# A graph network's attention hops: the first tile of every group gathered by TensorE from the table in SBUF instead of by an indirect DMA

## The reference, cut to what matters

```
h = concat(emb[head], emb[tail]) @ fc_w.T + fc_b
e = leaky_relu(sum(h * relation_emb[type]), slope 0.2)
w = softmax of e over the edges of each head
emb = sum over the edges of a head of w * emb[tail]  + emb
emb = emb / norm(emb)
```

## Time and profile before

| | us |
|---|---|
| time, median of 3 runs | 8048.83 (8046.11 to 8049.55) |
| the profiled execution: time | 8066.15 |
| the profiled execution: span | 8064.3 |
| TensorE busy (matmul) | 5613.4 (70%) |
| VectorE busy | 5187.3 (64%) |
| ACT busy | 1729.5 (21%) |
| GpSimd busy | 5810.4 (72%) |

### The profile page before, as it was taken

One profiled execution on the slowest core, in us unless ns is written; L12 is line 12 of the kernel. 1 busy time (PEld: TensorE's weight loads), 2 busy tenths in 40 slices (PEclk: granted clock), 3 DMA queues, 4 the chain that ended last, 5 costly groups with the idle time before them and its releaser, 6 DMA issues. The chain is left out here.

```text
span 8064.3 us, 179296 instructions
## 1 busy us (share of the span) xinstructions
PE 5613.4 (70%) x42094; PEld 3878.4 (48%) x42095; DVE 5187.3 (64%) x25581; ACT 1729.5 (21%) x3898; POOL 5810.4 (72%) x5647
## 2 busy tenths in 40 slices
PE   0991699999001477777777767777777777488885
PEld 0110111111000377766777656777777676366664
DVE  6888655555001577777777767777777777555555
ACT  2000000000000233333333323333333333122221
POOL 0888877777777577777777747777777777277775
PEclk9995899999555555555555555555555555588997
DMA  2992577776001333333323333323333333233332
GB/s 68 305 309 62 152 245 244 243 244 206 4 4 21 84 79 79 79 79 78 78 79 79 78 62 80 79 78 79 79 79 78 79 79 79 36 68 68 69 69 53
DMA packets 494534, 828.90 MB, mean 103 GB/s; under 512 B 225634, under 2 KB 379257, under 8 KB 445197
## 3 DMA queue, kind: packets, MB, share of 16 engines
q10 hardware_dynamic: 76307, 411.51, 15.4%
q0 software_dynamic: 180560, 257.90, 15.0%
q1 hardware_dynamic: 237610, 158.84, 7.9%
HBM read 800.05 MB, written 19.90 MB: 102 GB/s over the span
## 5 line engine op out<-in xcount | busy, mean ns | idle before, releaser
L1133 POOL DMA_INDIRECT rows<-tab_d,stage_idx x3264 | 3105.5, 951 | 1102.6 <-issue 992.0
L218 POOL DMA_INDIRECT rec_d<-stage_rec,stage_row x1600 | 1957.3, 1223 | 673.3 <-issue 662.3
L1183 PE MATMUL ps_g<-rows,prob 128*128 128x65 f32 x6528 | 1571.7, 419 | 8.9 <-issue 3.8
L427 PE MATMUL ps_gate<-ring,h_sb 128*1 128x512 f32 x3072 | 1488.4, 593 | 0.2 <-issue 0.2
L1183 PEld LDWEIGHTS ps_g<-rows,prob 128*128 128x128 f32 x6528 | 1440.8, 325 | 70.9 <-issue 40.2
L1467 POOL DMA_INDIRECT y_rows<-y_d,stage_src x768 | 736.6, 959 | 372.6 <-issue 217.7
L1149 PE MATMUL ps_turn<-ident_b,s_parts 128*128 128x128 bf16 x816 | 233.3, 286 | 972.8 <-DVE s_parts L1276 972.3
L1164 PE MATMUL ps_p<-ident_f,prob_t 128*128 128x128 f32 x3264 | 876.5, 423 | 0.0
L628 DVE TENSOR_SCALAR lo_hot<-iota_b,lo_t 128x128 bf16<-128x128 bf16 x1568 | 484.7, 324 | 461.1 <-PE ps_deg L438 439.5
L1264 DVE SCALAR_TENSOR_TENSOR picked<-iota_f,typ_e,x_sum 128x50 f32<-128x50 f32 x3264 | 698.5, 270 | 123.6 <-DVE x_sum L1261 107.5
L1241 DVE CUSTOM_DVE_ANT_0 masked<-lower,ps_s,m_old 128x512 f32<-128x512 bf16 x816 | 610.3, 748 | 162.5 <-DVE m_old L1239 155.0
(11 more groups left out here) (290 smaller groups left out, 6874.1 us busy)
## 6 DMA issues: line engine op xcount, KB each, us to landing
ring<-w_ih ACTq DMA_DIRECT2D x192, 1024.0 KB
ring<-w_hh ACTq DMA_DIRECT2D x192, 1024.0 KB
lo_wide<-lo_d SPq DMA_DIRECT2D x816, 128.0 KB
rows<-tab_d,stage_idx POOLq DMA_INDIRECT x3264
rec_e<-list_lo_d SPq DMA_DIRECT2D x216, 128.0 KB
rec_d<-stage_rec,stage_row POOLq DMA_INDIRECT x1600
y_rows<-y_d,stage_src POOLq DMA_INDIRECT x768
rec_d<-blank ACTq DMA_DIRECT2D x1, 3584.0 KB, 32.6
```

Of the source, the lines that this page charges most:

```text
L218: pool.indirect_dma_start(out=rec_d, out_offset=bass.IndirectOffsetOnAxis(ap=stage_row[:, h, j:j + 1], axis=0), in_=stage_rec[:, h, j, :], ...
L427: mm = pe.matmul(ps_gate[:, s, :], lhsT=h_sb[:, kc:kc + 1], rhs=ring[:, pc % RING, q, :], start=(kc == 0), stop=(kc == KC - 1))
L1133: pool.indirect_dma_start(out=rows[:, h * 4 + g, k, :], out_offset=None, in_=tab_d[hop], in_offset=bass.IndirectOffsetOnAxis(ap=stage_idx[ ...
L1183: mm = pe.matmul(ps_g[:, p, 0:C + 1], lhsT=prob[:, p, k * P:(k + 1) * P], rhs=rows[:, u, k, 0:C + 1], start=(k == 0), stop=(k == KT - 1))
```

## The change

In both hops the first tile of each group is no more fetched by an indirect DMA. The table's 115 used columns are kept in SBUF as three bf16 parts too (`t_parts`, built in `Tables`). In the stage before the hops VectorE finds, for each group, the first block of tails that its first tile reaches (`group_first`), and codes each tail relative to it: the place in the block plus 128, times a power of two for the block, in four scaled copies, stored beside the index rows in `lo_d` (so `lo_wide` has two rows, 256 KB). It also finds how many sweeps of four blocks (`GW`) the widest group takes (`n_near`).

In a hop VectorE compares the four code rows with the code of each partition, which gives the one-hots of four blocks at once (`hot_near`), in an inner loop over the sweeps. TensorE zeroes the accumulator `ps_t` and adds 4 blocks x 3 parts of the table in the same inner loop (`gather`), and ACT copies the result into the first tile of `rows`. The zeroing matmul and the gather are first in TensorE's order.

Further: scores stay float32, one operation instead of five, and are spread by four float32 turns of a broadcast column. ACT makes the mask, by Abs with a scale and a bias. All scores are negated, so that the running maximum is a minimum and the exponential takes it as its bias. There is one more lag, the index rows are asked for four groups ahead over two semaphores, and several buffers are laid over memory that is free by then.

```diff
-LAGS = (0, 1, 2, 3, 4)
+LAGS = (0, 1, 2, 3, 4, 5)
-LO_AHEAD = 3
+LO_AHEAD = 4
-PER_GROUP = 12
+PER_GROUP = 8
...
+    GW = 4
+    TW = C + 1 + R
+    MAX_NEAR = -(-NB // GW)
+    NBW = MAX_NEAR * GW
...
@@ Tables.vector @@
+    for lo, hi in ((0, half_cut), (half_cut, NB)):
+        t = tab[:, lo:hi, 0:TW]
+        rest = ...
+        link(dve.tensor_copy(t_parts[:, lo:hi, 0, :], t))
+        link(dve.tensor_tensor(rest, t, t_parts[:, lo:hi, 0, :], ALU.subtract))
+        link(dve.tensor_copy(t_parts[:, lo:hi, 1, :], rest))
+        link(dve.tensor_tensor(t_parts[:, lo:hi, 2, :], rest, t_parts[:, lo:hi, 1, :], ALU.subtract))
...
@@ the stage before the hops @@
+    for w in range(MAX_NEAR):
+        link.mark(dve.tensor_scalar(node_code[:, w:w + 1], part_f[:], float(P), 2.0 ** (GW * w), ALU.add, ALU.mult))
...
+    link(dve.scalar_tensor_tensor(out=near_rows[:, :, 0, :], in0=near_lo, scalar=float(P), in1=near_i.bitcast(F32),
+                                  op0=ALU.add, op1=ALU.mult))
+    for w in range(1, GW):
+        link.mark(dve.tensor_scalar(near_rows[:, :, w, :], near_rows[:, :, 0, :], 2.0 ** -w, None, ALU.mult))
...
@@ SP in a hop @@
-    wait_tick(sp, tick, lo_in, g * 16)
-    wait(sp, lower_rdy, g - 7)
-    sp.dma_start(lo_wide[:, u % 8, :], lo_d[ds(g, 1), :].broadcast_to([P, GE])).then_inc(lo_in, 16)
+    wait_tick(sp, tick, lo_in[u % 2], rows_in(g, u) - 16)
+    wait_tick(sp, tick, lower_rdy, g - 7)
+    wait(sp, hot_t_rdy, g - 7)
+    sp.dma_start(lo_wide[:, u % 8], lo_d[:, ds(g, 1), :].rearrange("v g e -> g v e")
+                 .broadcast_to([P, 2, GE])).then_inc(lo_in[u % 2], 16)
...
@@ GpSimd in a hop @@
-    for k in range(KT):
+    for k in range(1, KT):
...
@@ TensorE in a hop @@
+    def gather(g, first):
+        wait(pe, kept, g)
+        pe.matmul(ps_t[:, 0:TW], lhsT=zero_t[:], rhs=zero_t[:, 0:TW], start=True, stop=True,
+                  skip_group_check=True)
+        with pe.bass.Fori(0, sweeps, 1, engines=(pe.engine,)) as w:
+            at = pe.snap(pe.bass.s_assert_within(first + w * GW, 0, NBW - GW, ...))
+            pe.wait_ge(near_rdy, sweeps * g + (w + 1))
+            for b in range(GW):
+                for j in range(3):
+                    mm = pe.matmul(ps_t[:, 0:TW], lhsT=hot_near[:, b, :],
+                                   rhs=t_parts[:, ds(at + b, 1), j, :].rearrange("p a c -> p (a c)"),
+                                   start=False, stop=(j == 2), skip_group_check=True)
+            mm.then_inc(gathered, 1)
     def spread(g, p):
-            mm = pe.matmul(ps_s[:, p, k * P:(k + 1) * P], lhsT=pick_k[:, k, :], rhs=s_rows[:, p, :], ...)
+            mm = pe.transpose(ps_s[:, p, k * P:(k + 1) * P],
+                              score[:, p, k:k + 1].broadcast_to([P, P]), ident_f[:])
...
+    def body(i, u, stages, block_of, first_of):
+        _, z, a, s, _, c = stages
+        if z: gather(i - 1, first_of(1))
+        if s: spread(i - 3, (u - 3) % 2)
+        if c: turn_prob(i - 5, (u - 5) % 2)
+        if a: scores(i - 2, u % 2, (u - 2) % 8, block_of(2))
+        if c: sums(i - 5, (u - 5) % 2, (u - 5) % 8)
...
@@ ACT in a hop: the order is copy of the gathered tile, copy of the probabilities, exponential, mask @@
+        if z:
+            act.wait_ge(gathered, act_sweeps * g + (act_sweeps + 1))
+            act.activation(rows[:, v, 0, 0:TW], ps_t[:, 0:TW], ACT.Copy).then_inc(kept, 1)
...
+            act.activation(lower[:, (u - 1) % 4, :], lo_wide[:, (u - 1) % 8, 0, :], ACT.Abs,
+                           bias=far_bias[:], scale=BIG).then_inc(lower_rdy, 1)
...
@@ VectorE in a hop: masked minimum, m_diff, m_run, hot_t, x_sum, picked, score, hot_near, acc @@
+            link(dve.tensor_tensor_reduce(masked[:, p, :], lower[:, (u - 4) % 4, :], ps_s[:, p, :], 1.0,
+                                          m_old[:, p:p + 1], ALU.add, ALU.min, m_new[:, p:p + 1]))
+            dve.tensor_tensor(m_diff[:, p:p + 1], m_new[:, p:p + 1], m_old[:, p:p + 1], ALU.subtract
...
+            g, q = i - 2, u % 2
+            wait(dve, kept, g + 1)
+            wait(dve, landed[(u - 2) % 8], (g - (u - 2) % 8) * (PER_LAND // 8) + PER_LAND)
             wait(dve, x_rdy, g + 1)
...
+            dve.scalar_tensor_tensor(out=score[:, q, :], in0=s_raw[:, q, :], scalar=0.2,
+                                     in1=s_raw[:, q, :], op0=ALU.mult, op1=ALU.min).then_inc(score_rdy, 1)
+        if w:
+            wait(dve, lo_in[u % 2], rows_in(i, u))
+            dve.sem_inc(dtick, 1)
+            with dve.bass.Fori(0, sweeps, 1, engines=(dve.engine,)) as t:
+                dve.wait_ge(gathered, sweeps * i + (t + 1))
+                dve.tensor_scalar(hot_near[:].rearrange("p b e -> p (b e)"), lo_wide[:, u % 8, 1, :],
+                                  node_code[:, ds(t, 1)], None, ALU.is_equal).then_inc(near_rdy, 1)
```

More of the change, by code:

```diff
@@ L88, with pipelined @@
 BLOCK_LEAD = 8
-LAGS = (0, 1, 2, 3, 4)
+LAGS = (0, 1, 2, 3, 4, 5)
 LAG = LAGS[-1]
 UNROLL = 8
-LO_AHEAD = 3
-def pipelined(eng, n, body, table=None, top=0, link=None):
+LO_AHEAD = 4
+def pipelined(eng, n, body, tables=(), link=None):
     def steps(i0, count, flags):
-        v = blocks_from(eng, table, i0, UNROLL if count == UNROLL else 0, top) if table is not None else None
+        found = [(blocks_from(eng, table, i0, UNROLL if count == UNROLL else 0, top, back), back)
+                 for table, top, back in tables]
         for u in range(count):
-            body(i0 + u, u, flags(u), (lambda d, u=u: v[BLOCK_BACK + u - d]))
+            body(i0 + u, u, flags(u), *((lambda d, u=u, v=v, back=back: v[back + u - d]) for v, back in found))
     steps(0, UNROLL, lambda u: tuple(u >= lag for lag in LAGS))
@@ L202, in gnn_kernel @@
         tick = sem("tick")
-        staged = [sem(f"staged{h}") for h in range(2)]
+        staged = sort_staged = [sem(f"staged{h}") for h in range(2)]
+        idx_ld = sem("idx_ld")
+        piece_ld = [sem(f"piece_ld{i}") for i in range(RING)]
+        STAGED_BEFORE, PIECES_BEFORE, IDX_BEFORE = ES // 32 * 32, 2 * RC * (PC // RING) * 16, 3 * 16
         scattered = [sem(f"scattered{h}") for h in range(2)]
@@ L917, in _ @@
                     mm.then_inc(turned_rdy, 1)
+                    if r == 1:
+                        pe.wait_ge(near_in, 1)
+                        for c in range(4):
+                            mm = pe.transpose(ps_near[0:GN, c, :], dst0[:, c * GN:(c + 1) * GN], ident_f[:])
+                        mm.then_inc(near_out, 1)
+                pe.wait_ge(near_in, 2)
+                for j, v in enumerate((first4, last4)):
+                    for c in range(4):
+                        mm = pe.transpose(ps_first[:, j, c * GN:(c + 1) * GN], v[:, c:c + 1].broadcast_to([GN, P]),
+                                          ident_f[0:GN, 0:GN])
+                mm.then_inc(near_out, 1)
                 pe.wait_ge(to_turn, 3)
@@ new lines, in gather @@
+                        def gather(g, first):
[3 more added lines that the diff above has]
+                            with pe.bass.Fori(0, sweeps, 1, engines=(pe.engine,)) as w:
+                                at = pe.snap(pe.bass.s_assert_within(
+                                    first + w * GW, 0, NBW - GW, skip_runtime_bounds_check_because=
+                                    "the first block is held so low that the last sweep ends in the table"))
+                                pe.wait_ge(near_rdy, sweeps * g + (w + 1))
+                                for b in range(GW):
+                                    for j in range(3):
+                                        mm = pe.matmul(ps_t[:, 0:TW], lhsT=hot_near[:, b, :],
+                                                       rhs=t_parts[:, ds(at + b, 1), j, :]
+                                                       .rearrange("p a c -> p (a c)"),
+                                                       start=False, stop=(j == 2), skip_group_check=True)
+                                mm.then_inc(gathered, 1)
@@ L1178, in sums @@
                         def sums(g, p, u):
-                            wait(pe, landed[u], (g - u) * 8 + 64)
+                            wait(pe, landed[u], (g - u) * (PER_LAND // 8) + PER_LAND)
                             wait(pe, prob_rdy, g + 1)
@@ L1418, in gnn_kernel @@
                                    "gathered", "got_rdy", "win_rdy", "spread_out", "tab_new"))
-            staged = [seml(f"staged_y{h}") for h in range(2)]
+            staged = sort_staged
             landed = landed_y
-            lo_in = [seml(f"list_lo_in{i}") for i in range(3)]
+            lo_in = piece_ld[0:3]
             AHEAD = 5
```

273 lines of the change are left out of this document (158 added, 115 removed).

## The result

| | before | after |
|---|---|---|
| time, median of 4 runs each, us | 8048.64 (8046.11 to 8049.55) | 9985.21 (9984.70 to 9986.38) |
| ratio, 95% interval | | 1.2407 (1.2385 to 1.2428) |
| span of the profiled execution | 8064.3 | 9984.6 |
| TensorE, VectorE, GpSimd busy, us | 5613, 5187, 5810 | 7265, 4951, 5030 |
| x_sum, first to last start, us | 2712.9 to 6901.2 | 2735.6 to 8833.3 |

The change makes the kernel 24% slower; 7600 us was predicted, with a range that ended at 8120. All of it but 11 us lies in the stretch from the first to the last x_sum (6097.7 us instead of 4188.3).

What follows compares the result with a forecast made beforehand. GpSimd's gathers were taken to bound the hops at 5.03 us a group; the new cycle gives 4.46. 8066 - 460 + 11 = 7617, less 17 for the median, so 7600 us; eight-in-ten range 7330 to 8120.

Steps and rivals of the forecast that it cites:

- one sweep: Inner loop in the hops: one sweep of four blocks holds the first 128 edges of every group.
- no table loads on ACT in a hop: ACT's mask by Abs needs no table of its own; the rival of table switches, 8100 to 8450 us, had 0.03.
- the cycle named: In a hop: hot_near waits for the previous group's scores, TensorE's gather follows, and the next x_sum waits for its scores.
- x_sum to score: VectorE's stretch from x_sum to score in each group, a term of the cycle: 1.41 us.
- the sum of the cycle: Per group in the hops, VectorE and TensorE terms at the high clock: 4.21 us, 4.46 with loop edge and clock dips.
- TensorE's gather at 12 x 0.05 = 0.60 us: Cycle term at the high clock: 12 of 13 matmuls, the zeroing being ahead of the wait.
- 2.4 GHz nearly throughout: TensorE's clock in the hops: high with dips at loop edges, granted clock above 0.85; dips cost 0.05 us a group.
- slow rival: TensorE's clock stays low in the hops: 6.07 us a group with the edge, about 8900 us; chance 0.10.
- o: Inner loop setup on VectorE between score and the comparison hot_near: 0.30 us a group.
- the handover to TensorE: Cycle term from VectorE's comparison to TensorE's gather: 0.05 us a group.
- The loop edge: Edge of the unrolled loop in the hops: 1.6 us once in eight groups, 0.20 us a group.
- Outside the hops: Table parts before hop 2 cost 3 us, one more pipeline step per hop 8 us, preparation of codes 0: 11 us.

Runs made afterwards that it cites:

- The filler: Changed kernel with the gather's zeroing matmul issued 13 times instead of once, in TensorE's gap before the gather: 9229 us, 1.146 of the kernel before.
- the repaired kernel: Changed kernel with hot_near ahead of x_sum in VectorE's order and register table loads in fours, everything computed: 7826 us, 0.972 of the kernel before.

## Why the prediction was wrong, point by point

**Right.** GpSimd was the bound before; one sweep; no table loads on ACT in a hop; the other parts of the change free; the cycle named, its members and what each waits for. x_sum to score took 1.42 us (1.41 forecast), and the index rows land 3.4 us after their issue (median), asked for four groups ahead (`LO_AHEAD`; the prediction has seven), and hold up nothing.

**The step that failed first: the sum of the cycle, TensorE's gather at 12 x 0.05 = 0.60 us.** It takes 1.83 in the changed kernel and 1.81 with the clock high. With a fixed address it takes 0.65. I took the price of a matmul from the four of the spread (ps_s), whose addresses are fixed, halved it for the high clock, and gave it to each of the 12 gather matmuls, which has a run-time address of its own. They start 0.13 us apart at either clock, and the spread follows 0.35 us behind the last one (0.13 with the inner loop written out, so 0.22 of the 1.83 is the loop's). The price also hangs on the place. In the kernel with hot_near first, in the 200 of 284 groups (3000 to 4500 us) where the sums are still running ahead of the gather and the clock is high, the first five or six gather matmuls start 0.05 us apart and the rest 0.12 to 0.14, with single steps up to 0.20. The filler's run has both prices in one kernel, 1.81 us behind a wait and 1.25 without one. That the address work is done ahead of time where the queue is full, and not where it stands at a wait, is my reading; it fits all of these numbers.

**The clock.** "2.4 GHz nearly throughout" followed from 5.57 us of TensorE work in a 4.46 us group. But the cycle leaves a gap whenever VectorE's score stretch is longer than the sums, and TensorE's work has to fit between. In 120 of 201 groups the clock stayed low; in the rest the high level stood at the sums and the gap, and the part that the cycle waits for was low but for short stretches. The filler prices this: spread, turn, scores and their handover 2.58 us low, 1.50 high, 1.08 us a group. My slow rival had the sign and this part of the mechanism, with a chance of 0.10, and was still 1070 us short, as it had the gather at 1.24, the inner loops at 0.30 and the edge at 0.20 a group. The Trainium skill (TensorE: Matmul & The Clock Gate, Part 1, "HAM oscillation") tells of a kernel whose batches of matmuls, with a DMA wait between them, each start at the low clock. The trace has the same outcome behind shorter waits as well (0.2 to 1.2 us inside a pass): spread and turn stood at 0.50 in all 201 groups. The rule that I did weigh, that turns keep the full clock from engaging (the Trainium skill, the same page, Part 4), is not what happened: with eight turns a group the repaired kernel has 0.94.

**The inner loops.** o was 0.30 us from score to hot_near; it is 0.48 to 0.59, and the handover to TensorE 0.23 instead of 0.05. Both include what I left out: o also holds score's own 0.16, and TensorE's loop has a setup of its own (with it written out the handover is 0.14). Together they are 0.47 us above the forecast in the group shown.

**The loop edge.** Forecast 1.6 us a pass, as the earlier trace rows; it is 3.75 (10.7 less 6.9), 0.47 a group instead of 0.20. I took for granted that a load of 9 to 13 entries costs what one of 12 does; the start of the load decides. The Trainium skill (Runtime: NRT & Kernel Launch, Instruction fetch mechanics) gives about 200 ns a register for a TENSOR_LOAD, even in bulk; it speaks of loads from HBM, and these tables lie in SBUF. The loads of the changed kernel are near that (2.40 us for 10, 0.24 each), those of the kernel before are not (0.85 for 12, 0.07 each).

The terms add up: gather +1.23, clock +1.08, loops +0.47 and x_sum to score +0.01 make the 7.00 us of the group shown out of 4.21; the mean inside a pass is 6.9, and with the edge's 0.47 it is the 7.4 measured.

**Outside the hops.** Forecast +11 us. Hop 1's first gather starts 14.5 us later (2721.1; the earlier trace rows), so the preparation was not free. Before hop 2's first gather GpSimd idles 104.05 us instead of the 83.34 of the earlier trace rows, 20.7 more. This is not the table: its parts take 19.5 us on VectorE, and the next loads of indices are issued 20.8 us after their start, against 19.4 us from the same point to the same load in the kernel before (4818.41 to 4837.83). So they are hidden but for 1.4 us, where I had 3 (its own 20.8 less 18.8 is 2). The rest is the end of hop 1: its last x_sum starts 28 us after GpSimd's last gather ended, 9 before, as one more group is in flight then and each takes 7 us.

```profile
5815.15 0.94 POOL L1229 DMA_INDIRECT rows<-tab_d,stage_idx  x1 [104.05 <-DMA stage_idx<-dst_e]
```

```profile
5791.85 1.60 DVE L754 CAST t_flat<-tab 128x2760 bf16<-128x2760 f32 x1
...
5812.62 1.16 SPq L1193 DMA_DIRECT2D stage_idx<-dst_e  x2
```

**The thing not asked.** The prediction named a closed cycle through the gather and costed it, but did not ask whether the comparison had to stand in it. It does not: hot_near needs only the index row and the gather before it. One block moved was worth 1731 us, part of it by the clock, more than any term that I had weighed.

## What to carry to other kernels

When work goes to an engine that takes part in a cycle, price it at the place where it stands and ask first whether it can stand ahead of the cycle's wait; here the same gather cost 2.1 us a group more behind score than ahead of x_sum. Price matmuls with run-time addresses and loads of registers by rows of the same form, not by rows of the same shape. And where TensorE's clock is in doubt, look at it inside one group: a mean of 0.59 was 0.50 in three groups of five and, in the others, a high level that fell on the sums, beside the cycle.

## What the runs showed of the hardware

- A load of block numbers into registers takes 0.85 us for 12 and 1.10 for 13 or 16 entries when it begins on a multiple of four entries, and 1.94 (8), 2.07 to 2.17 (9), 2.40 (10), 2.89 (12) and 2.96 us (13) when it does not, on both TensorE and VectorE.
- Bf16 matmuls of 115 columns, each with a run-time address, started 0.13 us apart behind a wait at either clock, against 0.054 with fixed ones at the high clock. Behind zeroing matmuls without a wait they started 0.097 us apart at the low clock, which is what fixed ones take there (0.094 to 0.097).
- Thirteen zeroing matmuls in place of one in a gap made the program 756 us faster: nothing but added work, and the granted clock in the hops went from 0.59 to 0.93. A small part of the gain is the shorter gather behind the loop edge.
- What the repaired kernel is worth differed with the chip: 6.8% on one where the kernel before takes 9908 us, 2.8% on one where it takes 8052. Whether the chip itself is the cause is not shown.
